# One opening stage for setup, SwiGLU and key fold, and mask products of the last retrieval block among the output products of the one before

## The reference

```
expert = argmax(onehot, axis=-1)                  # one of 8 experts per sequence
up, gate = x @ W_up[expert].T + b_up, x @ W_gate[expert].T + b_gate
y = (silu(up) * gate) @ W_down[expert].T + b_down       # 512 hidden units
xn = y * rsqrt(mean(y * y) + 1e-6) * norm_w
q = xn @ w_q.T                                    # 8 heads, 2 halves of 128
sim1, sim2 = q[half 0] . keys[0], q[half 1] . keys[1]   # 64 keys each
# top 8 of each half, the 64 sums, top 8 of those: 64 of 4096 experts per token
h = gelu(xn . expert_down[chosen]) * relu(score)
x = x + sum(h * expert_up[chosen])
```

## Time and profile before

| | us |
|---|---|
| median of three runs | 1929.24 |
| the profiled execution | 1929.26 |
| its span, first to last instruction | 1927.6 |
| TensorE busy | 1757.1 |
| VectorE busy | 943.0 |
| ScalarE busy | 374.6 |
| GpSimd busy | 305.4 |
| first retrieval product begins at | 153.48 |
| first product of the stage behind the retrieval begins at | 861.14 |

### The profile page before, as it was taken

How to read it: one execution, slowest core, us unless ns; L and a number is a source line. 1 busy time by engine, 2 the same in 40 slices (tenths; PEclk the granted TensorE clock), 3 DMA queues, 4 the chain that set the end, 5 groups by cost and what they waited for, 6 DMA issues and landing times. The chain is left out here.

```text
span 1927.6 us, 32039 instructions
## 1 busy us (share of the span) xinstructions
PE 1757.1 (91%) x13350; PEld 1097.1 (57%) x13350; DVE 943.0 (49%) x2520; ACT 374.6 (19%) x635; POOL 305.4 (16%) x150
## 2 busy tenths in 40 slices
PE   5879789999999999778799998999999976998998
PEld 2347678887888888764344443444444455447443
DVE  1326888768687785407311111111114497236676
ACT  2222111120111201001011111111113639133200
POOL 0000413151331514200394000000000000004000
PEclk9988899999999999789899999999999988999999
DMA  7000000000000000025310001200001044000000
GB/s 305 33 0 6 2 2 8 2 9 8 2 8 2 9 7 3 8 79 232 150 47 1 0 0 73 123 0 0 0 0 55 0 155 139 6 0 1 6 17 22
DMA packets 20043, 73.33 MB, mean 38 GB/s; under 512 B 3530, under 2 KB 8130, under 8 KB 17090
## 3 DMA queue, kind: packets, MB, share of 16 engines
q1 hardware_dynamic: 19906, 71.37, 9.9%
HBM read 69.26 MB, written 2.10 MB: 37 GB/s over the span
## 5 line engine op out<-in xcount | busy, mean ns | idle before, releaser
L563 POOL TENSOR_TENSOR peer_bm<-peer_bm,peer_slots 128x512 f32<-128x512 f32 x64 | 193.9, 3029 | 609.1 <-DVE peer_bm L650 609.1
L436 PE MATMUL peer_ps_h<-all_x,layer_down 128*128 128x256 f32 (+1 forms) x1024 | 241.3, 390 | 0.4 <-issue 0.4
L474 PE MATMUL peer_ps_o<-peer_hg,layer_up 128*128 128x256 f32 x1024 | 226.6, 382 | 1.5 <-DVE peer_hg L682 1.5
L474 PEld LDWEIGHTS peer_ps_o<-peer_hg,layer_up 128*128 128x128 f32 x1024 | 195.9, 192 | 33.3 <-issue 5.2
L436 PEld LDWEIGHTS peer_ps_h<-all_x,layer_down 128*128 128x128 f32 x1024 | 192.9, 193 | 28.4 <-issue 2.5
L1129 DVE SCALAR_TENSOR_TENSOR skills_hid<-skills_ps_u,all_pair_w,skills_act_g 128x512 f32<-128x512 f32 x64 | 48.0, 751 | 294.7 <-PE skills_ps_u L1091 294.7
L451 PE MATMUL peer_ps_w<-peer_bm,peer_am 64*64 64x32 f32 x8192 | 144.5, 227 | 31.9 <-DVE peer_hg L682 25.1
L451 PEld LDWEIGHTS peer_ps_w<-peer_bm,peer_am 64*64 64x64 f32 x8192 | 137.1, 144 | 52.1 <-issue 52.1
L508 ACT ACTIVATE peer_hg<-peer_ps_h 128x512 f32<-128x512 f32 x128 | 76.4, 597 | 371.7 <-PE peer_ps_h L436 371.7
L652 DVE TENSOR_TENSOR peer_am<-all_iota_a,peer_slots 128x2048 f32<-128x2048 f32 x64 | 146.2, 2285 | 0.0
L1108 ACT ACTIVATE skills_act_g<-skills_ps_g 128x512 f32<-128x512 f32 x96 | 57.3, 597 | 438.0 <-PE skills_ps_g L1091 438.0
(11 more groups left out here) (288 smaller groups left out, 2228.0 us busy)
## 6 DMA issues: line engine op xcount, KB each, us to landing
quant_w<-in_l_w SPq DMA_DIRECT2D x64, 256.0 KB, 4.3
lora_w<-in_l_w SPq DMA_DIRECT2D x8, 1024.0 KB, 8.7
four_skill<-in_skills SPq DMA_DIRECT2D x2, 3072.0 KB, 12.9
skills_w<-in_skills SPq DMA_DIRECT2D x2, 3072.0 KB, 15.1
skills_w<-in_skill_shared SPq DMA_DIRECT2D x2, 3072.0 KB, 22.0
layer_down<-in_down SPq DMA_DIRECT2D x1, 4096.0 KB, 24.3
layer_up<-in_up SPq DMA_DIRECT2D x1, 4096.0 KB, 33.5
swiglu_w<-in_cond SPq DMA_DIRECT2D x2, 1541.0 KB, 8.2
```

The lines of the kernel that those rows point to most:

```text
L436: mm = pe.matmul(ps_h[group % 2][:, r, :], down[:, c, j * P:(j + 1) * P], g.x[:, c, bass.ds(i * PB, PB)], start=(c == 0), stop=(c == C - 1))
L474: mm = pe.matmul(ps_o[:, c, :], up[:, j, c * P:(c + 1) * P], hg[half][:, j, :], start=(j == 0), stop=(j == NJ - 1))
L563: pool.tensor_tensor(bm[c % RING][:], bm[c % RING][:], slots[half][:, 2, c * PAIRS:(c + 1) * PAIRS].unsqueeze(2).to_broadcast([P, PAIRS, WJ]),
```

## The change

`setup`, `swiglu` and `keys_fold` become one stage `begin` with one block. The loads of x are four, one per token block, the first issued in the setup part. Each sequence has its own weight buffer, loaded in two parts. The order on TensorE is written out without loops: the fold's products of a quarter (512 columns) stand, in two parts, between a block's gate products and its down products, and the mean of block q stands behind the second group of block q + 1. ScalarE's square root and VectorE's normalisation move with it.

```
+def begin(nc, a, g):
+        w = [sb(f"w{b}", [P, COND0 + COND0_BIAS]) for b in range(B)]
+        ps_f = ps("ps_f", [P, BLK])
...
+            def load_x(q):
+                sp.dma_start(x[:, :, blocks[q]], a["x"][:, :, blocks[q]]).then_inc(xload[q], 16)
+            def load_w(b):
+                e = sp.value_load(g.best[0:1, b * 8:b * 8 + 1], min_val=0, max_val=E8 - 1)
+                of = a["cond0"][bass.ds(e, 1), :, :].rearrange("a p n -> p (a n)")
+                sp.dma_start(w[b][:, 0:2 * C * H0], of[:, 0:2 * C * H0]).then_inc(in_load[b], 16)
+                sp.dma_start(w[b][:, 2 * C * H0:COND0 + COND0_BIAS],
+                             of[:, 2 * C * H0:COND0 + COND0_BIAS]).then_inc(out_load[b], 16)
...
+            load_x(0)
+            sp.dma_start(norm_w[:], a["norm_w"]).then_inc(nload, 16)
+            sp.wait_ge(d, 7)
+            load_w(0)
+            load_x(1)
+            sp.dma_start(g.wq[:], a["wq"]).then_inc(key_load, 16)
+            sp.dma_start(g.keys[:], a["keys"]).then_inc(key_load, 16)
+            load_x(2)
+            load_w(1)
+            load_x(3)
+            sp.dma_start(g.down[:], a["down"]).then_inc(ahead, 16)
+            sp.dma_start(g.up[:], a["up"]).then_inc(ahead, 16)
...
+            def normalise(q):
+                dve.wait_ge(ms_done, q + 1)
+                dve.reciprocal(rms[:], ms[:]).then_inc(rms_done, 1)
...
+            def keep_fold(r):
+                dve.wait_ge(folded, r + 1)
+                dve.tensor_copy(g.key_map[:, r // 2, (r % 2) * BLK:(r % 2 + 1) * BLK], ps_f[:]).then_inc(copied, 1)
+            for q in range(NBLK):
...
+                for m in range(M0):
...
+                    if m == 1 and q > 0:
+                        normalise(q - 1)
+                keep_fold(q)
+            normalise(NBLK - 1)
...
+            for q in range(NBLK):
+                pe.wait_ge(xload[q], 16)
+                if q % BPB == 0:
+                    pe.wait_ge(in_load[q // BPB], 16)
+                for m in range(M0):
+                    entered(q, m)
+                    if m == 1 and q > 0:
+                        mean(q - 1)
+                if q == 0:
+                    pe.wait_ge(key_load, 32)
+                    pe.wait_ge(pair_ready, 2)
+                fold(q, 0)
+                if q + 1 < NBLK:
+                    fold(q, 1)
+                left(q)
+            fold(NBLK - 1, 1)
+            mean(NBLK - 1)
```

In `peer`, TensorE's `work(NPB - 2, last=True)` puts `weigh` of the last block among its own output products, one ahead of every eighth:

```
                 for c in range(C):
                     for j in range(NJ):
+                        if last and j % (C * NJ // CHUNKS) == 0:
+                            weigh(i + 1, (c * NJ + j) * CHUNKS // (C * NJ))
                         mm = pe.matmul(ps_o[:, c, :], up[:, j, c * P:(c + 1) * P], hg[half][:, j, :],
...
-            work(NPB - 1, 1, more=False, route=False)
+            work(NPB - 2, 0, last=True, route=False)
+            pe.wait_ge(p_done, NPB * CHUNKS + 1)
+            pe.wait_ge(x_done, NPB - 1)
+            for c in range(C):
+                for j in range(NJ):
+                    mm = pe.matmul(ps_o[:, c, :], up[:, j, c * P:(c + 1) * P], hg[1][:, j, :], start=(j == 0), stop=(j == NJ - 1))
+            mm.then_inc(o_ready, 1)
...
-                    if c == 0 and not first:
+                    if c == 0 and not first and not last:
                         add_out(i - 1)
...
+            add_out(NPB - 2)
             add_out(NPB - 1)
```

More of the change, by code:

```diff
@@ L108, in setup @@
         ones_row = sb("ones_row", [1, P])
[L109 to L116, removed]
+        x = sb("x", [P, C, T])
+        w = [sb(f"w{b}", [P, COND0 + COND0_BIAS]) for b in range(B)]
+        w_up = [t[:, 0:C * H0].rearrange("p (c h) -> p c h", c=C) for t in w]
@@ new lines, in begin @@
+        sq = sb("sq", [P, C, BLK])
+        ms = sb("ms", [P, BLK])
+        rms = sb("rms", [P, BLK])
+        ps_u = [ps(f"ps_u{i}", [P, BLK]) for i in range(2)]
+        ps_g = [ps(f"ps_g{i}", [P, BLK]) for i in range(2)]
+        ps_d = ps("ps_d", [P, C, BLK])
+        ps_v = ps("ps_v", [P, BLK])
+        ps_f = ps("ps_f", [P, BLK])
+        cond_load, nload, ahead = sem("cond_load"), sem("nload"), sem("ahead")
+        xload = [sem(f"xload{q}") for q in range(NBLK)]
+        in_load = [sem(f"in_load{b}") for b in range(B)]
@@ L188, in _ @@
                 act.activation(ex[:, e], shifted[:, e], ACT.Exp, accum_out=total[:, b:b + 1]).then_inc(exp_done, 1)
[L190 to L216, removed]
@@ new lines, in deviation @@
+            def deviation(q):
+                act.wait_ge(ms_ready, q + 1)
+                act.activation(ms[:], ps_v[:], ACT.Sqrt, bias=g.eps[:, 0:1]).then_inc(ms_done, 1)
+            act.wait_ge(consts, 4)
+            for q in range(NBLK):
+                b = q // BPB
+                act.wait_ge(out_load[b], 16)
+                for m in range(M0):
+                    n = q * M0 + m
+                    act.wait_ge(up_ready, n + 1)
+                    if q > 0:
+                        act.wait_ge(hid_done, n - M0 + 1)
+                    act.activation(su[:, m, :], ps_u[m % 2][:], ACT.Silu, bias=b_up[b][:, m:m + 1]).then_inc(su_done, 1)
+                    if m == 1 and q > 0:
+                        deviation(q - 1)
+                if q > 0:
+                    act.wait_ge(xn_done, q * C)
+                for c in range(C):
+                    act.wait_ge(down_ready, q * C + c + 1)
+                    act.activation(xc[:, c, :], ps_d[:, c, :], ACT.Identity, bias=b_down[b][:, c:c + 1]).then_inc(xc_done, 1)
+                    act.wait_ge(xc_done, q * C + c + 1)
+                    act.activation(sq[:, c, :], xc[:, c, :], ACT.Square).then_inc(sq_done, 1)
@@ L453, in weigh, with work @@
                 mm.then_inc(w_ready, 1)
-            def work(i, half, first=False, more=True, route=True):
+            def work(i, half, first=False, last=False, route=True):
                 for c in range(CHUNKS):
                     weigh(i, c)
-                    if more:
-                        if first and c % CPT == 0:
-                            scores(i + 1, c // CPT)
-                        for group in range(c * GPC, (c + 1) * GPC):
-                            act_rows(i + 1, group)
-                            if first and group == NGRP // 2 + 1:
-                                turn(i + 1, 0)
-                            if not first and group == 2:
-                                turn(i + 1, 1)
+                    if first and c % CPT == 0:
+                        scores(i + 1, c // CPT)
+                    for group in range(c * GPC, (c + 1) * GPC):
+                        act_rows(i + 1, group)
+                        if first and group == NGRP // 2 + 1:
+                            turn(i + 1, 0)
+                        if not first and group == 2:
+                            turn(i + 1, 1)
                 if route:
```

209 lines of the change are left out of this document (87 added, 122 removed).

## The result

The changed kernel has a median of 1878.2 us over four runs (1874.93 to 1881.66), before 1930.07: a ratio of 0.9739 with a 95% interval of 0.9717 to 0.9761. That is 51.9 us faster by the medians and 50.4 by the ratio. The forecast was 1873.7, its range 1866 to 1886. The profiled execution took 1879.65 with a span of 1877.8, 49.8 under the span of before.

What follows compares the result with a forecast made beforehand. TensorE, busy 91%, was taken to bound the kernel through its waits and clock. Opening 35.8 and retrieval end 19.8 sum to 55.6 us, taking 1929.26 to 1873.7, range 1866 to 1886.

Steps and rivals of the forecast that it cites:

- Start: Kernel start: expert weights issued at about 5.75, so the first SwiGLU product begins at 11.1, 9.8 us earlier.
- Stops and second expert: Opening stage: filled stops ahead of down products (4.6 less 0.3) and means (5.1), second weight buffer 6.9 us.
- Fold: Seven fold parts before the last down product add 6.0 us, at 0.107 a pass as in lora's product.
- The rival of the low clock: Opening stage: fold loads hold TensorE at clock 0.50 and slow the products behind; 1887 us, chance 9%.
- Landing in turn: Early loads land in issue order, the first expert's up and gate part at 10.9; opposing rival 1882 us, 6%.
- Behind the last down product: From the last down product to the first scores 10.6 us are left of 26.3, 15.7 less.
- End: End of the retrieval: eight weigh-and-output pairs, one wait and last products take 73.9 us against 93.7, 19.8 less.
- in the retrieval it is fed without a break until 786.22: Retrieval before the change: TensorE was taken to have no stops until the last block's eight mask chunks.
- what follows is the same code, shifted: Code behind the retrieval's changed end: taken as merely earlier, with no term for a change in its time.

Runs made afterwards that it cites:

- mean_at_end: Changed kernel, but each token block's mean, root and normalisation stand at the block's end again; one execution, 1880.5 us, first scores at 123.39.
- second_late: Changed kernel, but the second expert's two loads are issued only when the first expert's blocks are biased; one execution, 1884.6 us, first scores at 126.91.
- fold_together: Changed kernel, but all 64 fold passes stand ahead of block 0's down products; one execution, 1891.4 us, first scores at 130.62.
- no_loop: Changed kernel, but TensorE's loop over blocks 1 to 4 of the retrieval is written out; ratio to before 0.9734, 1879.1 us.
- code_moved: Changed kernel plus 128 long-fulfilled waits of TensorE where it stands idle behind the last mean; ratio to before 0.9716, median 1874.6 us.

## Why the prediction was right

- **Start, 9.8 us.** First product at 10.77 (11.1 forecast): 10.1 us.
- **Stops and second expert.** 4.3 + 5.1 + 6.9 us were forecast. Up to the last down product all stops are gone but one of 0.27 (fold part at 98.47, down products at 99.60; 0.3 forecast). The last down product streams until 106.5 (107.0 forecast). `mean_at_end` prices the mean's place at 5.0, `second_late` the buffer at 10 in the new order. That the first scores were 0.7 us ahead of the forecast of 117.7 is luck: in the other executions they stand 0.3 to 0.9 behind it.
- **Fold, 6.0 us.** 16 passes in 1.73, 0.108 each; the row of `lora` was the right neighbour. The rival of the low clock has its truth: `fold_together` lost it in the third quarter. The Trainium skill's rule for a weight load ("TensorE: Matmul & The Clock Gate", section on LDWEIGHTS: columns divided by 1.2, in ns) agrees with 0.108 at the high clock and again not with the 0.22 of that kernel's fourth quarter.
- **Landing in turn.** Held: in all fourteen traces the loads of the first 130 us land in the order of their issue. It is no rule of the queue. In the quantised feed-forward, pieces of 256 KB land out of turn, in `no_loop` by 1.75 us: issued at 1506.79 and 1508.15, landed after 6.5 and 3.4 us, at 1513.34 and 1511.59.

```profile
quant_w<-in_l_w SPq DMA_DIRECT2D x1, 256.0 KB, 6.5
...
quant_w<-in_l_w SPq DMA_DIRECT2D x1, 256.0 KB, 3.4
```

  The Trainium skill ("DMA: Bandwidth & Descriptors", section on two DMAs through the same engine) says that nothing orders DMAs across the engines. It says what can't be relied on, not, as the prediction read it, that the expert's weights would land late; the pieces of 256 KB agree with it.
- **Behind the last down product, 10.6 us.** 10.5 (106.5 to 116.96).
- **End, 19.8 us.** 19.8, with the pitch of 5.65 and the stop of 0.95.
- **What is missing.** 4.5 us by the medians, 5.8 by the spans of the profiled executions. The step that failed is the prediction's treatment of the unchanged code: "in the retrieval it is fed without a break until 786.22", which the trace of before contradicts (1.78 us at 469.14, 1.79 at 638.71), and "what follows is the same code, shifted", with no term for it. 3.7 us went in the retrieval ahead of the changed end and 2.9 behind it, against 0.7 gained on the opening. `code_moved` shows that the place of the code alone is worth 6.4 us in the retrieval. The 2.9 us behind it are not shown to come from the change: with the same instructions that stretch takes 1065.2 to 1070.4 us in the fourteen traces, 1068.0 in the repetition of the changed kernel and 1065.2 in `fold_together`, which has the new opening too. Part of the missing time is thus scatter of single executions.

## What to carry to other kernels

A product that waits for another engine should have independent work of TensorE beside it, from the next or the last block; read the pitch of such a pair from where the kernel already has it, and the forecast holds to a few tenths. Short passes that are bound by weight loads cost half among dense ones, so hand them out in small portions. When stages are rewritten, compare also the stages that were not: streams of very short matmuls can lose microseconds by the place of their instructions, and a run with the code moved, or the list of instruction transfers beside the idle times, tells that from a real loss. And before a difference of a microsecond in a stage is given a cause, compare a repetition of the same kernel.

## What the runs showed that was not expected

- A stop of under 2 us in a stream of short instructions can cost more than itself: 1.84 us of idle time, with stops of 0.78 and 1.70 in the 10 us before, made one chunk 4.6 us longer, since the clock went to 1.2 GHz with it. 0.97 us, with 1.73 behind it, did not (`code_moved`).
- Idle times that nothing else ends stand where a 16 KB transfer of TensorE's own instructions lands too late. They keep to the same few chunks in the kernels with the new opening and the loop, with the loads of `xin` moved or not, and move with 128 instructions put ahead.
- VectorE stands still for 3.2 to 3.5 us where its loop branches back, in every trace; TensorE feels it once in the retrieval, for 3.1 to 3.2 us when it has no idle time of its own there.
- The same eight mask chunks took 36.0 us in one kernel and 43.0 in another (755.77 to 798.74), by the chunk in which the clock fell and by stops of 0.3 us.
